# A separate minimum for each half of the attention scores, and one small instruction that combines them

## The reference

```python
content = jnp.einsum('bihd,bjhd->bhij', q + u_bias, k)
pos = jnp.einsum('bihd,jhd->bhij', q + v_bias, p)
pos = _relative_shift(pos)
attn = jax.nn.softmax((content + pos) * scale, axis=-1)
head = jnp.einsum('bhij,bjhd->bihd', attn, v).reshape(B, S, Dm)
```

## Time and profile before

| | us |
|---|---|
| median of 3 runs | 3433.29 (3432.21 to 3438.11) |
| the profiled execution | 3432.96 |
| its span, first to last instruction | 3431.2 |
| TensorE busy (modelled ends) | 3357.4 (98%) |
| TensorE weight loads | 2081.5 (61%) |
| ScalarE busy | 2329.2 (68%) |
| VectorE busy | 1941.3 (57%) |
| GpSimd busy | 1326.9 (39%) |
| DMA moved | 1231.27 MB, 359 GB/s over the span |

### The profile page before, as it was taken

One profiled execution on the slowest core, in us unless ns is written; L12 is line 12 of the kernel. 1 busy time (PEld: TensorE's weight loads), 2 busy tenths in 40 slices (PEclk: granted clock), 3 DMA queues, 4 the chain that ended last, 5 costly groups with the idle time before them and its releaser, 6 DMA issues. The chain is left out here.

```text
span 3431.2 us, 110393 instructions
## 1 busy us (share of the span) xinstructions
PE 3357.4 (98%) x34876; PEld 2081.5 (61%) x34876; DVE 1941.3 (57%) x5651; ACT 2329.2 (68%) x3255; POOL 1326.9 (39%) x1341
## 2 busy tenths in 40 slices
PE   8996999999999999999999999999999999999988
PEld 5662566666666666666666666666666666666677
DVE  7771555555555555555555555555555555555557
ACT  3342777777777777777777777777777777777633
POOL 2110444444444444444444444444444444444400
PEclk9996999999999999999999999999999999999999
DMA  5977999999999999999999999999999999999862
GB/s 165 293 246 242 379 390 388 389 390 387 387 387 392 387 388 388 390 388 388 388 389 390 387 387 390 389 387 389 389 389 388 387 388 391 388 388 388 303 197 98
DMA packets 433554, 1231.27 MB, mean 359 GB/s; under 512 B 48993, under 2 KB 133473, under 8 KB 433505
## 3 DMA queue, kind: packets, MB, share of 16 engines
q1 hardware_dynamic: 430000, 1229.12, 95.6%
q10 hardware_dynamic: 3504, 1.53, 0.2%
HBM read 617.04 MB, written 613.43 MB: 359 GB/s over the span
## 5 line engine op out<-in xcount | busy, mean ns | idle before, releaser
L867 POOL TENSOR_SCALAR at_pos_in<-at_pos_in,at_neg_max 128x1024 f32<-128x1024 f32 x1024 | 1145.8, 1119 | 1660.4 <-DVE at_neg_max L830 1660.4
L792 ACT ACTIVATE at_pos_out<-at_ps_pos 128x1024 f32<-128x1024 f32 x1024 | 1049.2, 1025 | 530.8 <-PE at_ps_pos L704 530.8
L830 DVE CUSTOM_DVE_ANT_0 at_pos_in<-at_ps_con,at_pos_in 128x512 f32<-128x512 f32 x1024 | 708.3, 692 | 1188.8 <-PE at_ps_con L704 818.5
L704 PE MATMUL at_ps_con<-at_right,at_left 32*128 32x512 f32 x4096 | 1329.5, 641 | 0.0
L801 ACT ACTIVATE at_prob<-at_ps_turn 128x512 f32<-128x512 f32 x2048 | 1111.5, 595 | 283.1 <-PE at_ps_turn L737 241.8
L704 PE MATMUL at_ps_pos<-at_right,at_left 32*128 32x512 f32 x4096 | 1167.4, 646 | 33.6 <-DMA at_left<-scratch_queries 20.6
L737 PE MATMUL at_ps_turn<-keep_ident,at_pos_in 128*128 128x128 f32 x8192 | 1105.9, 278 | 0.0
L737 PEld LDWEIGHTS at_ps_turn<-keep_ident,at_pos_in 128*128 128x128 f32 x8192 | 890.6, 141 | 156.5 <-issue 154.9
L750 PEld LDWEIGHTS at_ps_pv<-at_prob,at_v_aug 128*32 128x32 f32 x16384 | 385.0, 109 | 773.6 <-issue 773.5
L830 DVE CUSTOM_DVE_ANT_0 at_pos_in<-at_ps_con,at_pos_in,at_neg_half 128x512 f32<-128x512 f32 x1024 | 768.7, 751 | 140.5 <-PE at_ps_con L704 6.1
L750 PE MATMUL at_ps_pv<-at_prob,at_v_aug 128*32 128x128 f32 x16384 | 659.3, 279 | 0.8 <-issue 0.8
(11 more groups left out here) (92 smaller groups left out, 1387.6 us busy)
## 6 DMA issues: line engine op xcount, KB each, us to landing
scratch_scores<-at_pos_out SPq DMA_DIRECT2D x1024, 512.0 KB, 7.3
at_pos_in<-scratch_scores SPq DMA_DIRECT2D x1024, 512.0 KB, 7.5
scratch_queries<-fr_qk SPq DMA_DIRECT2D x128, 256.0 KB, 3.9
at_left<-scratch_queries SPq DMA_DIRECT2D x127, 256.0 KB, 7.3
fr_x<-in_L_attn_x_dram SPq DMA_DIRECT2D x16, 512.0 KB, 7.1
scratch_x<-fr_x_bo SPq DMA_DIRECT2D x16, 512.0 KB, 4.9
scratch_keys<-fr_qk SPq DMA_DIRECT2D x32, 256.0 KB, 5.2
scratch_values<-fr_values SPq DMA_DIRECT2D x8, 1024.0 KB, 5.8
```

The source lines that it names most:

```text
L704: return pe.matmul(banks[:, n, :], left[side][rows, t.i * P:(t.i + 1) * P], right[side][rows, :], start=True, stop=True)
L792: act.activation(pos_out[:, t.slot, :], ps_pos[:, :, :].rearrange("p a m -> p (a m)"), ACT.Copy)\
L830: dve.tensor_tensor_reduce(pos_in[:, t.slot, keys], ps_con[:, n, :], pos_in[:, t.slot, keys], -SCALE, 3.0e38 if n == 0 else neg_half[:, t. ...
L867: pool.tensor_scalar(pos_in[:, t.slot, :], pos_in[:, t.slot, :], -1.0, neg_max[:, t.slot:t.slot + 1], ALU.mult, ALU.add).then_inc(shifted, 1)
```

## The change

Each half now takes its minimum from the same large start value and writes it to its own column of `neg_half`, which gets a second column. The second half no longer waits for the first one's `scored`. Then VectorE waits for both halves with a nop, and a `tensor_tensor` of 128 x 1 takes the smaller of the two columns into `neg_max` and signals a new semaphore, `lowest`. GpSimd's subtraction waits for `lowest` and not for `scored`. TensorE waits for `scored` as before.

```diff
--- before.py
+++ after.py
@@ -553,7 +553,7 @@
 
         pos_out = sb("pos_out", [P, RING, S])
         pos_in = sb("pos_in", [P, RING, S])
-        neg_max, neg_half = sb("neg_max", [P, RING]), sb("neg_half", [P, RING])
+        neg_max, neg_half = sb("neg_max", [P, RING]), sb("neg_half", [P, RING, 2])
         prob = [sb(f"prob{k}", [P, TILES, QUAD * P]) for k in range(2)]
         left = [sb(f"left{k}", [P, S]) for k in range(2)]
         right = [sb(f"right{k}", [P, HALF]) for k in range(2)]
@@ -568,9 +568,9 @@
         written, read = sems("written", RING), sems("read", RING)
         q_in, k_in, vals_in, head_out = (sems(n, 2) for n in ("q_in", "k_in", "vals_in", "head_out"))
         first_in, p_ready = sem("first_in"), sem("p_ready")
-        (pos_mm, pos_copied, con_mm, scored, shifted, turned, exped, pv_mm, pv_copied, head_mm, inverted,
+        (pos_mm, pos_copied, con_mm, scored, lowest, shifted, turned, exped, pv_mm, pv_copied, head_mm, inverted,
          normed, v_ready, cleared, blanked) = (
-            sem(n) for n in ("pos_mm", "pos_copied", "con_mm", "scored", "shifted", "turned", "exped",
+            sem(n) for n in ("pos_mm", "pos_copied", "con_mm", "scored", "lowest", "shifted", "turned", "exped",
                              "pv_mm", "pv_copied", "head_mm", "inverted", "normed", "v_ready", "cleared", "blanked"))
 
         class Tile:
@@ -823,13 +823,12 @@
                         dve.wait_ge(read[t.slot], t.rounds(RING, 1))
                         if t.past(RING):
                             dve.wait_ge(shifted, t.count(1, 1 - RING))
-                    else:
-                        dve.wait_ge(scored, t.count(2, 1))
                     dve.nop(nofuse=True)
-                    low = neg_half if n == 0 else neg_max
                     dve.tensor_tensor_reduce(pos_in[:, t.slot, keys], ps_con[:, n, :], pos_in[:, t.slot, keys], -SCALE,
-                                             3.0e38 if n == 0 else neg_half[:, t.slot:t.slot + 1], ALU.add, ALU.min,
-                                             low[:, t.slot:t.slot + 1]).then_inc(scored, 1)
+                                             3.0e38, ALU.add, ALU.min, neg_half[:, t.slot, n:n + 1]).then_inc(scored, 1)
+                at_once(dve, scored, t.count(2, 2))
+                dve.tensor_tensor(neg_max[:, t.slot:t.slot + 1], neg_half[:, t.slot, 0:1], neg_half[:, t.slot, 1:2],
+                                  ALU.min).then_inc(lowest, 1)
 
             def copy_products(t):
                 dve.wait_ge(pv_mm, t.quads(1))
@@ -863,7 +862,7 @@
         @block.gpsimd
         def _(pool):
             def less_maximum(t):
-                at_once(pool, scored, t.count(2, 2))
+                at_once(pool, lowest, t.count(1, 1))
                 pool.tensor_scalar(pos_in[:, t.slot, :], pos_in[:, t.slot, :], -1.0, neg_max[:, t.slot:t.slot + 1],
                                    ALU.mult, ALU.add).then_inc(shifted, 1)
```

## The result

The changed kernel took 3483.69 us (median of 4 runs, 3478.91 to 3485.92) against 3433.32 for the kernel before (4 runs): a ratio of 1.0142, 95% interval 1.0125 to 1.016. The forecast was 3341 us, with a range of 3290 to 3415.

A forecast was written before the change was run, and what follows sets the result against it. TensorE and VectorE by turns bound the kernel at 2.847 us per tile; compute would reach 2.72, but DMA holds it at 2.76. That saves 89 us, rounded to 92: 3433 − 92 = 3341 us, range 3290 to 3415.

The forecast's parts named there:

- What bounds the kernel now: In the middle of the run, TensorE and VectorE set the pace by turns, 2.85 us per tile against 2.847 measured.
- The loop of 2.65 and 3.00 us: Two tiles alternate between TensorE's 2.65 us and VectorE's 3.00: 5.65 us, 2.825 each, plus 0.03 for the heads.
- Parts 1 to 3: On VectorE, an earlier second add (0.62 us after the first, not 0.83), 0.06 us shorter, giving 2.72 us per tile.
- VectorE's leg: From a tile's opening TensorE weight load to the next tile's second-half load, through VectorE's adds: 2.73 us instead of 3.00.
- Parts 4 and 5: VectorE's added nop and minimum (0.29 us per tile) are covered, and GpSimd's later-signalled shift has room: no cost.
- R1: Rival: compute alone decides, DMA carries 406 GB/s, 2.72 us per tile, 3303 us; chance 0.20.
- What is late next: DMA between score writes and read-backs binds next, at 400 GB/s: 2.76 us per tile instead of compute's 2.72.
- The room of some 4 us: Read-backs are issued 12.6 us ahead of the first add and land after 8.9 at most; this slack goes first.
- the 2.72 asked for: Compute's pace per tile after the change, down from 2.847 us, needing 406 GB/s from DMA.
- R4: Rival: pressed DMA gets worse, to 345 GB/s or half way, 367; 3.01 us per tile, 3600 us; chance 0.05.

The follow-up runs named there:

- e4: The kernel before, reading back only columns 0 to 767 of each row of positional scores: 3434.34 us.
- e3: The changed kernel, reading back only columns 0 to 767 of each row of positional scores: 3303.41 us.
- e12: The changed kernel, with SP issuing a tile's write only when the write of three tiles before has landed: 3494.96 us, ratio 1.0146 to the kernel before.
- e2: The changed kernel, but the second half again waits for the first, without taking its minimum as start value: 3480.27 us, ratio 1.0101 to the kernel before.
- e5: The changed kernel, each small transfer cut in two, the first part a multiple of 15 rows: slower, losing 0.05 us per tile.
- e6: The kernel before, each small transfer cut in two, the first part a multiple of 15 rows: slower, losing 0.05 us per tile.
- e8: The changed kernel, the load of queries cut into 63 rows and 1 row: 97 us slower than the changed kernel on the same chip.
- e10: The changed kernel, all four small transfers cut into a multiple of 7 rows and a rest: over 3500 us.
- e14: The changed kernel, reading back 896 of 1024 columns of positional scores: 3345.55 us.
- e16: The changed kernel, loading only one of each pair of equal query strips, GpSimd copying it to the other: 3462.67 us.
- e7: The changed kernel, writing the scores in plain row order (WRITE_GAPS 4 becomes 1): 3709.26 us, ratio 1.0621.
- e1: The changed kernel, but the second half again waits for the first and starts from its minimum: 3457.36 us, ratio 1.0038 to the kernel before.

## Why the prediction was wrong, step by step

- **What bounds the kernel now**: right. The loop of 2.65 and 3.00 us explained 2.847, and e4 shows that DMA did not set this pace.
- **Parts 1 to 3, VectorE's leg**: right to the hundredth: 0.62 us, 0.69 us, and, in e3, 919 tiles in 2500 us, 2.72 each.
- **Parts 4 and 5, the additions at no cost**: right (e3 takes 3303.41 us against R1's 3303), and the shift is never late.
- **What is late next**: the mechanism was foreseen. The room of some 4 us was used up, then the first add waited for its read and DMA set the pace. The step that failed is the rate given to DMA: "What they carry is at least 395 … I take the middle between the rate seen and the rate asked for, 400 GB/s: 2.76 us per tile". Pressed, they carried 380, and a tile took 2.904 us. The step held two errors. First, 395 was not a higher rate. TensorE's records are 567 in those 50 us and 5668 in the 500 us of the earlier trace rows (the others are in the earlier trace rows), the same pace; and 7 GB/s over 50 us are 0.35 MB, less than one transfer of 0.5 MB, so the window's edges make the difference. Secondly, a rate that is served while nothing is pressed was taken as a floor. A stretch too short to fill the room says what was asked for and not what can be carried: the same 50 us of the changed kernel show 406 GB/s, with landings that climb. Two figures could have warned: the spread of landings by engine (the 16th increment 1.3 us behind the 15th even before), and the packets. The median 4 KB packet took 0.159 us in the kernel before. A DMA engine has 16 of them per tile and 0.15 to 0.17 us of small transfers, which is an estimate of 2.70 to 2.71 us for an engine with no slow packet at all, against the 2.72 asked for.
- **R4**, at 0.05, was what happened: below 388 GB/s once pressed. Its rates of 345 to 367 GB/s were far too low (it forecast 3600 us), and I gave it little since I had it rest on the start of the phase alone. The range had no room for it; an outcome on the slow side of 3433 deserved more than a twentieth, since no row showed DMA pressed.
- **The Trainium skill's two figures** (DMA: Bandwidth & Descriptors): the 358 GB/s of Where 436 GB/s comes from is passed by both kernels here, with 388 and 380 over 500 to 3000 us; the 425 of Measured, for a core alone, is not reached by this mix of reads and writes on one queue (406 at best over 50 us). The forecast lay between them and was still too high.

What stays open: why the late engine takes 2.90 us per tile once pressed while the kernel before kept up at 2.847 on the chip of the result. e12 excludes the backlog as such. The kernel before itself shows both: 3433 and up to 3488 us, depending on chip and run; on the two chips where it never keeps up (3465 us and more) the plain change was not measured. A difference between chips or placements, and contention from fifteen engines whose work comes in bursts when SP is released, both remain possible; neither was tried. Nor is it shown which engine it is, or why it is slower than its neighbours.

## What to carry to other kernels

Before a loop is made faster, ask what rate its transfers would then need, and look per engine: a transfer ends with its slowest share, so that one late engine of sixteen can bind while the sum of rates and the busy share look the same. If this rate is above what a long stretch has shown (long enough to fill all the buffers between the engines), run the faster version with fewer bytes once; beside a run with all its bytes it tells what compute is worth and what DMA takes back. When DMA binds, take bytes or packets off it: 1.5% of the bytes brought the kernel before 1.1% on the chip where it fell behind. And do not count on staying where you were: with 0.27 us less on VectorE in each tile, and DMA pressed, this kernel lost 1.4%.

## What the runs showed of the hardware that I had not expected

- One share of 16 came 5 to 7 us after all others in every profile in which DMA was pressed all along (the changed kernel three times, e2, e5, e6, e8 to e10, e14, e16), and 0.3 us after them with a quarter of the reads left out (e3). By e5 and e6 it is an engine among the eight that an 8-row transfer uses and not among the four of a 4-row one. It took about 2.9 us per tile for 16 packets of 4 KB and, by my estimate, 0.17 us of small transfers; the median packet of all engines took 0.159 us.
- Row order of the same writes: 353 GB/s in plain order (e7) against 380 interleaved by four.
- Rows split into two dimensions were dealt out as if they were one: 63 rows given as 7 x 9 went to nine engines, 28 as 7 x 4 and 126 as 7 x 18 to fourteen (e8, e10).
- An add that follows an accumulator read on VectorE starts together with it even when it uses the same accumulator (1506.46 and 1506.46). The start value from a tile costs 60 ns: the second add took 751 ns with it (e1) and 691 without (e2, the same kernel but for that); in the changed kernel it takes 686.
